# Nine-tap grouped convolutions by phases: the last convolution's partial shifts as 32x32 tiles in float32

## The reference, cut to what matters

```python
x = x + conv9(x, w0, groups=4, pad=4) + ctx0(c)[:, :, None] + side[None, :, None]
x = x + mixed(x, c, mix1)   # per sample: (sum_k att[k] * W[k]) @ x + (att @ bias_k)[:, None]
x = x + mixed(x, c, mix2)   # att = softmax of a small gelu network of the condition c
x = x + conv9(x, w3, groups=4, pad=4) + ctx3(c)[:, :, None] + side[None, :, None]
```

## Time and profile before

| | us |
|---|---|
| median of 3 runs | 631.91 |
| lowest, highest | 631.85, 632.3 |
| the profiled execution, its time | 635.33 |
| its span from first to last instruction | 633.5 |
| TensorE busy in it | 622.8 |
| VectorE, ScalarE, GpSimd busy | 500.9, 338.2, 272.3 |

### The profile page before, as it was taken

How to read it: one execution, slowest core, us unless ns; L and a number is a source line. 1 busy time by engine, 2 the same in 40 slices (tenths; PEclk the granted TensorE clock), 3 DMA queues, 4 the chain that set the end, 5 groups by cost and what they waited for, 6 DMA issues and landing times.

```text
span 633.5 us, 26750 instructions
## 1 busy us (share of the span) xinstructions
PE 622.8 (98%) x11938; PEld 506.3 (80%) x11938; DVE 500.9 (79%) x1002; ACT 338.2 (53%) x626; POOL 272.3 (43%) x163
## 2 busy tenths in 40 slices
PE   8999999999999999999999999999999999999995
PEld 6888897777788777889877778777878877788874
DVE  6899777978777887887887887797877788788735
ACT  4665455555455456455456446555545545645534
POOL 4133454354355345355435345435435534534220
PEclk8999999999999999999999999999999999999998
DMA  8066665557765556775555776555776555655515
GB/s 244 24 188 215 203 211 177 204 163 225 232 207 156 190 176 199 232 232 158 173 191 175 232 232 182 158 202 162 223 232 208 155 190 176 201 169 168 161 76 201
DMA packets 50572, 118.84 MB, mean 188 GB/s; under 512 B 5621, under 2 KB 26282, under 8 KB 42714
## 3 DMA queue, kind: packets, MB, share of 16 engines
q1 hardware_dynamic: 49170, 116.04, 58.1%
q0 software_dynamic: 576, 1.26, 0.5%
q10 hardware_dynamic: 776, 0.89, 0.4%
HBM read 35.33 MB, written 33.55 MB: 109 GB/s over the span
## 4 chain that ended last, share of the span: by engine, by line
PE 96%; DMA 2%; DVE 1%; ACT 1%; issue 0%; ACTq 0%; DVEq 0%
PE ps L1068 45%; PE ps L1079 19%; PE ps L1090 16%; PE ps L1214 14%; PE ps L1192 1%; DMA out_sb<-in_L_cond_weight 1%; DMA out_planes<-out_taps 1%; ACT out_sb L740 1%; PE ps L1262 0%; PE ps L1185 0%; DVE out_taps L856 0%; DVE x_in L950 0%; DVE x_hi L993 0%; PE ps L1250 0%; PE ps L1302 0%
## 5 line engine op out<-in xcount | busy, mean ns | idle before, releaser
L513 POOL COPY out_sb<-out_planes 128x2048 f32<-128x2048 f32 x30 | 123.0, 4099 | 187.8 <-issue 162.0
L496 POOL COPY x_full<-x_in 128x2048 f32<-128x2048 f32 x29 | 117.1, 4038 | 113.9 <-DVE x_lo L822 110.1
L846 DVE SCALAR_TENSOR_TENSOR z_lo<-ps,bias_tab,z_hi 128x1024 fp32r<-128x1024 f32 x62 | 76.7, 1279 | 60.7 <-ACT z_hi L649 60.7
L1090 PE MATMUL ps<-x_full,taps_raw 32*32 32x512 f32 x2880 | 102.2, 598 | 0.0
L1068 PEld LDWEIGHTS ps<-z_hi,taps_hi 32*128 32x128 f32 x1488 | 71.0, 183 | 35.4 <-issue 25.1
L1068 PE MATMUL ps<-z_hi,taps_lo 32*128 32x512 f32 x1488 | 96.5, 387 | 0.0
L836 DVE SCALAR_TENSOR_TENSOR y_lo<-ps,bias_tab,y_hi 128x512 fp32r<-128x512 f32 x128 | 87.2, 744 | 10.2 <-ACT y_hi L639 10.2
L1068 PE MATMUL ps<-z_hi,taps_hi 32*128 32x512 f32 x1488 | 94.2, 396 | 0.0
L657 ACT ACTIVATE out_taps<-ps,bias_tab 128x512 f32<-128x512 f32 x62 | 39.3, 685 | 102.2 <-PE ps L1068 102.2
L1068 PE MATMUL ps<-z_lo,taps_hi 32*128 32x512 f32 x1488 | 90.3, 385 | 0.0
L1214 PE MATMUL ps<-y_hi,mix_w 32*128 32x512 f32 x1024 | 88.0, 385 | 0.0
(11 more groups left out here) (158 smaller groups left out, 831.0 us busy)
## 6 DMA issues: line engine op xcount, KB each, us to landing
x_in<-in_x SPq DMA_DIRECT2D x31, 1024.0 KB, 5.3
out_planes<-out_taps SPq DMA_DIRECT2D x122, 256.0 KB, 3.6
out<-out_sb SPq DMA_DIRECT2D x30, 1024.0 KB, 4.6
mix_w<-prod SPq DMA_DIRECT2D x124, 128.0 KB, 4.0
x_in<-in_x SPq DMA_DIRECT2D x2, 512.0 KB, 5.9
out<-out_sb POOLq DMA_DIRECT2D x2, 512.0 KB, 3.5
out<-x_full SPq DMA_DIRECT2D x7, 128.0 KB, 2.9
out_taps<-in_L_cond_weight SPq DMA_DIRECT2D x1, 512.0 KB, 5.8
```

The source lines that it names most:

```text
L496: pool.tensor_copy(row_order(t, d, x[:, :, home(t, d)]), x_order(t, d, x_in[t.par(d)][:, :])).then_inc(x_planed, 1)
L513: pool.tensor_copy(x_order(t, d, out_sb[t.par(d)][:, :]), row_order(t, d, out_planes[:, :, :]))\
L846: dve.scalar_tensor_tensor(out=z_home(t, 0)[1][:, 2 * h:2 * h + 2, home(t, 0)], in0=ps[:, k:k + 2, :], scalar=bias_tab[:, b, 2 * G:BIAS], ...
L1090: tile = pe.matmul(ps[rows(p), first_bank + g, :], taps_raw[l][rows(g), d - p, :], full[rows(g), d % PH, c:c + S], start=False, stop=(n == ...
```

## The change

The partial shifts of conv3 take the form that conv0 has had: 18 whole turns, then 48 matmuls of 32x32 tiles in float32, for samples 1 to 30. In detail:

- `z_full`, a third copy of z in float32, unsplit. ScalarE writes it from PSUM in `whole_z`: two activations of 128x1024, each after the z_lo of its half, then, after both, two edge copies (3 phases each) and `z_full_edged`. It stands in `edges_z` between z_hi's edges and z_lo's; those now cover one phase each instead of four.
- `conv3_mixed` takes the place of `conv3` for t >= 2: 12 whole turns (LATER is 12), the product, 6 whole turns, the 48 small matmuls. At t = 31 mix(31) stands after the 12 turns.
- In `conv0_mixed`, before the last two of the 18 whole turns, TensorE now waits for `z_lo_done` and `z_full_edged` of sample t-1.
- The columns of conv3's weight tiles are in phase order (32 p + o) where they were 4 o + p; so the relay DMA reads 32 neighbouring partitions for each phase where it read every fourth.
- Sample 31 (`last_conv`) keeps the old column order. It needs its own tiles: after conv0(31) GpSimd zeroes `taps_hi[0]` and `taps_lo[0]` whole, ScalarE and VectorE fill them from `taps_raw[1]` (four instructions each, `last_taps_high` ahead of z_hi(31), `last_taps_low` ahead of z_lo(31)). Its bias is moved to the old order by four small DMAs of GpSimd at t = 16.

```diff
+        def full_z(t, d):
+            return not isinstance(t.half, int) or FIRST_FULL_Z <= t.i + d < N - 1
...
-                    sp.dma_start(out_planes[:, p, :], out_taps[p:C:PH, :, :]).then_inc(out_relaid, DMA)
+                    sp.dma_start(out_planes[:, p, :], out_taps[rows(p), :, :]).then_inc(out_relaid, DMA)
...
+            def zero_last_taps():
+                pool.wait_ge(conv0_done, G * N)
+                for w in (taps_hi[0], taps_lo[0]):
+                    pool.memset(w[:, :, :].bitcast(F32), 0.0).then_inc(last_taps_zeroed, 1)
...
             def edges_z(t):
                 for z, done in ((z_hi, z_hi_done), (z_lo, z_lo_done)):
+                    if z is z_lo and full_z(t, 0):
+                        whole_z(t)
                     act.wait_ge(done, 2 * (t.i + 1))
-                    for o, i in edges(z):
+                    for o, i in (edges(z, slice(PH - 1, PH), slice(0, 1)) if full_z(t, 0) else edges(z)):
                         last = act.activation(o, i.bitcast(F32), ACT.Copy)
                 last.then_inc(z_edged, 1)
+
+            def whole_z(t):
+                b = t.i
+                for h in range(2):
+                    act.wait_ge(z_lo_done, 2 * b + h + 1)
+                    k = bank(t, 0) + 2 * h
+                    act.activation(z_full[:, 2 * h:2 * h + 2, home(t, 0)], ps[:, k:k + 2, :], ACT.Identity,
+                                   bias=bias_tab[:, b, 2 * G:BIAS]).then_inc(z_full_done, 1)
+                act.wait_ge(z_full_done, 2 * (b + 1 - FIRST_FULL_Z))
+                for o, i in full_edges(z_full):
+                    last = act.activation(o, i, ACT.Copy)
+                last.then_inc(z_full_edged, 1)
...
-                whole_turns(bank(t, 0), 0, hi, lo, [(2, d) for d in far], step, False)
+                pe.wait_ge(z_lo_done, 2 * b)
+                pe.wait_ge(z_full_edged, b - FIRST_FULL_Z)
+                if t.at(2):
+                    pe.wait_ge(taps_raw_step[1], 2)
+                whole_turns(bank(t, 0), 0, hi, lo, [(2, d) for d in far], step)
                 if middle:
                     middle()
-                partial_turns(bank(t, 0), 0, full, conv0_done, step)
+                partial_turns(bank(t, 0), 0, full, step, done=conv0_done)
+
+            def conv3_mixed(t, turns, middle):
+                b = t.i - 1
+                order = [(k, d) for k in range(2) for d in WHOLE] + [(2, d) for d in WHOLE]
+                if t.at(2):
+                    pe.wait_ge(prod_summed, b + 2)
+                pe.wait_ge(z_edged, b + 1 - PLAIN)
+                whole_turns(bank(t, -1), 1, z_hi, z_lo, order[:turns], BLK, first=True)
+                middle()
+                whole_turns(bank(t, -1), 1, z_hi, z_lo, order[turns:], BLK)
+                partial_turns(bank(t, -1), 1, z_full, BLK, done=conv3_done)
...
-            MID = TURNS // 2
-            LATER = 20
+            LATER = 12
...
+                elif t.at(N - 1):
+                    conv3_mixed(t, LATER, lambda: mix(t))
+                else:
+                    conv3_mixed(t, LATER, lambda: product(t, 1))
                     mix(t)
```

More of the change, by code:

```diff
@@ L46 @@
 FIRST_MIXED = 2
+FIRST_FULL_Z = 1
 K = 8
@@ L85, in conditioned_residual_kernel @@
         z_lo = sb("z_lo", [C, PH, ROW], F32R)
+        z_full = sb("z_full", [C, PH, ROW])
         out_taps = sb("out_taps", [C, G, S])
@@ L372, in phase_columns, with last_columns @@
         def phase_columns(w, l, p):
-            view = w[l][:, p:p + TAPS, :]
-            return view[:, :, GC * p:GC * p + GC] if l == 0 else view[:, :, p:C:PH]
+            return w[l][:, p:p + TAPS, GC * p:GC * p + GC]
+        def last_columns(w, p):
+            return w[0][:, p:p + TAPS, p:C:PH]
         def rows(r):
@@ L580, in _ @@
                 pool.memset(buf[:, :, ROW - 1:ROW].bitcast(F32), 0.0).then_inc(far_zeroed, 1)
-            for buf in x_full:
+            for buf in x_full + [z_full]:
                 pool.memset(buf[:, :, 0:ROW:ROW - 1], 0.0).then_inc(far_zeroed, 1)
@@ L584, in _, with bias_for_last @@
             first_planes(ALL[1], 1)
+            def bias_for_last():
+                pool.wait_ge(bias_tab_done, 3)
+                for p in range(PH):
+                    pool.dma_start(bias_last[p:C:PH, :], bias_tab[rows(p), N - 1, G:2 * G]).then_inc(bias_last_in, DMA)
+            def zero_last_taps():
+                pool.wait_ge(conv0_done, G * N)
+                for w in (taps_hi[0], taps_lo[0]):
+                    pool.memset(w[:, :, :].bitcast(F32), 0.0).then_inc(last_taps_zeroed, 1)
             for t in ALL[2:N]:
@@ L587, in _ @@
                     end_rows(t.i - 1)
+                if t.i == N // 2:
+                    bias_for_last()
                 one(t)
+            zero_last_taps()
             store_woven(0)
@@ L664, in taps_high, with last_taps_high @@
                    .then_inc(taps_hi_done[l], 1)
+            def last_taps_high():
+                act.wait_ge(last_taps_zeroed, 2)
+                for p in range(PH):
+                    act.activation(last_columns(taps_hi, p), taps_raw[1][:, :, :], ACT.Copy).then_inc(last_taps_hi_done, 1)
             def spread_first():
@@ L719, in relay_last @@
                 for p in range(2, PH):
-                    act.dma_start(out_planes[:, p, :], out_taps[p:C:PH, :, :]).then_inc(out_relaid, DMA)
+                    act.dma_start(out_planes[:, p, :], out_taps[rows(p), :, :]).then_inc(out_relaid, DMA)
             def evac_last(h):
+                act.wait_ge(bias_last_in, PH * DMA)
                 for g in range(2, G):
@@ L940, in one, with last_taps_low @@
                     low_z(t)
+            def last_taps_low():
+                dve.wait_ge(last_taps_zeroed, 2)
+                for p in range(PH):
+                    dve.wait_ge(last_taps_hi_done, p + 1)
+                    dve.tensor_tensor(out=last_columns(taps_lo, p), in0=taps_raw[1][:, :, :],
+                                      in1=last_columns(taps_hi, p).bitcast(F32), op=ALU.subtract)\
+                       .then_inc(last_taps_lo_done, 1)
             def turn_last(h):
@@ L956, in bias_first_half @@
             def bias_first_half():
+                dve.wait_ge(bias_last_in, PH * DMA)
                 for g in range(2):
@@ L1071, in conv_turns, with whole_turns @@
                             tile.then_inc(done, 1)
-            def whole_turns(first_bank, l, hi, lo, turns, step, first):
+            def whole_turns(first_bank, l, hi, lo, turns, step, first=False, done=None):
                 for k, d in turns:
@@ L1078, in whole_turns, with partial_turns @@
                     for g in range(G):
-                        pe.matmul(ps[:, first_bank + g, :], w[rows(g), d, :], a[rows(g), d % PH, c:c + S],
-                                  start=(first and (k, d) == turns[0]), stop=False)
-            def partial_turns(first_bank, l, full, done, step):
+                        tile = pe.matmul(ps[:, first_bank + g, :], w[rows(g), d, :], a[rows(g), d % PH, c:c + S],
+                                         start=(first and (k, d) == turns[0]), stop=(done is not None and (k, d) == turns[-1]))
+                        if done is not None and (k, d) == turns[-1]:
+                            tile.then_inc(done, 1)
+            def partial_turns(first_bank, l, full, step, first=False, done=None):
                 for n in range(PARTIAL):
@@ L1090, in partial_turns @@
                             tile = pe.matmul(ps[rows(p), first_bank + g, :], taps_raw[l][rows(g), d - p, :],
-                                             full[rows(g), d % PH, c:c + S], start=False, stop=(n == PARTIAL - 1))
-                        if n == PARTIAL - 1:
+                                             full[rows(g), d % PH, c:c + S], start=(first and n == 0),
+                                             stop=(done is not None and n == PARTIAL - 1))
+                        if done is not None and n == PARTIAL - 1:
                             tile.then_inc(done, 1)
@@ L1104, in conv0_mixed @@
                 wait(pe, out_dve, 2 * (b - 1))
-                whole_turns(bank(t, 0), 0, hi, lo, [(k, d) for k in range(2) for d in near], step, True)
+                whole_turns(bank(t, 0), 0, hi, lo, [(k, d) for k in range(2) for d in near], step, first=True)
                 if not plain(t, 0):
                     pe.wait_ge(x_hi_edged, b + 1 - PLAIN)
-                whole_turns(bank(t, 0), 0, hi, lo, [(k, d) for k in range(2) for d in far], step, False)
+                whole_turns(bank(t, 0), 0, hi, lo, [(k, d) for k in range(2) for d in far], step)
                 if not plain(t, 0):
```

31 lines of the change are left out of this document (21 added, 10 removed).

## The result

The changed kernel takes 726.12 us (725.49 to 727.36, 3 runs) against 631.91; the ratio is 1.149, with a 95% interval of 1.147 to 1.151. It is 94 us slower, where 71 more were forecast; the range was 690 to 745.

A forecast was written before the change was run, and what follows sets the result against it. TensorE bounds the kernel, busy 622.8 of 633.5 us. Step 2 3.8, steps 3 to 30 64.7, step 31 2.2 and the relay 0.5 sum to 71.2; with 631.91, 703.1 us, range 690 to 745.

The forecast's parts named there:

- The two stalls: TensorE idles in each step, 2.17 us inside conv0 for z_full and 0.62 us at the product for y_lo.
- TensorE's own work: conv3 loses 18 turns and gains 48 small matmuls: 0.48 us a step less, 18.34 us from 18.82.
- The wait inside conv0: Before conv0's last two whole turns, TensorE stands from 3.63 to 5.80 us until z_full is complete: 2.17 us a step.
- The product's wait: In conv3, TensorE reaches the product at 12.57 us but y_lo allows it at 13.19: 0.62 us.
- The step, 21.13: Loop step from one conv0 start to the next: 21.13 us, 2.31 more than 18.82.
- Beginning: Step 2 costs 3.8 us more; from step 3 on, each step costs 2.31 us more.
- End: Step 31, conv0 to last_conv, takes 20.87 us, 2.2 more; the last relay takes 0.5 more.
- new tiles for sample 31: Tiles refilled after the last conv0 are ready by 15.5, ahead of z at 16: no cost, up to 1 us.
- The clock: TensorE's granted clock stays up, near 0.99, with both stalls: 52%, 692 to 715 us; its fall: 32%.
- a clock under 0.97: Sign in the profile afterwards that the forecast is wrong: TensorE's granted clock below 0.97.
- rival 1: TensorE's clock falls in the stalls, one step in two, 1.7 to 3.4 us each: 720 to 755 us, 32%.
- Rival 2: z_full's wait in conv0 is met in time, only the product is late: step 19.93, 664 us; about 10%.

The follow-up runs named there:

- run 3: Changed kernel with the z_full wait moved from conv0 to conv3 (except step 2) and the product behind all 18 whole turns; 628.82 us, ratio 0.995.
- run 8: Kernel before, with only the relay changed to read 32 neighbouring partitions for each phase; 633.31 us, ratio 1.0014.
- run 11: run 3 with sample 1 keeping conv3's old turns and the last relay's four DMAs shared out in another order; 627.58 us, ratio 0.993.
- run 10: Changed kernel with eight extra matmuls of 128x128x512 ahead of the wait in conv0, output not the reference's; 709.27 us.
- run 1: Changed kernel with TensorE waiting for z_full in conv3 and not inside conv0, step 2 keeping its wait; 669.49 us, ratio 1.060.
- run 4: Changed kernel with one more wait in conv0, four whole turns earlier, for the first half of z_full; 725.28 us.
- run 5: run 3 with the parts of the next sample's matrices behind y_hi and y_lo on ScalarE and VectorE; 658.28 us.

## Why the prediction was right or wrong, point by point

The measured time lies in the range, but not where the forecast had its centre: 726.1 against 703.1. The two stalls came as they were worked out; on top of them the clock fell, which the prediction had as its first rival, and the range held because that rival was in it. Of the 23 us between, some 18 are the falls, 3 the step, 1 step 3 and 1.6 the end behind `last_conv`.

- *TensorE's own work becomes 18.34 us a step.* Right: run 3 measured 18.52, with the product 0.13 late by its own timeline.
- *The wait inside conv0, resuming at 5.80.* Right, 5.79. The stall is 1.96 to 2.01 by the trace's idle time against the 2.17 of the working, since the modelled end of the matmul ahead of it lies inside the stall. What follows is P at 6.46 where 6.37 was worked out: two turns and the passage take 0.67 behind a stall, not 0.57.
- *The product's wait.* Right in kind and place: product at 13.21 against 13.19. Its idle time is 0.35, not 0.62, for the same reason.
- *The step, 21.13.* The quiet steps are 21.19 to 21.35, 21.25 on average. Over 28 steps the difference is some 3 us.
- *Beginning.* Step 2 cost 3.7 us (3.8 forecast), step 3 cost 3.2 (2.31). In step 3 z_hi starts 1.26 us after conv0 in place of 0.24: ScalarE stands at x_lo's edges until 72.62, because x_lo of step 2 is late, and conv0's stall is 2.98 us.
- *End.* conv0(31) to `last_conv` took 22.41, which is 20.9 and one fall; 20.87 was forecast. The relay was taken at 0.5 more; it is longer by 2.7 in the trace, of which run 8 accounts for 1.9, and the end behind `last_conv` is longer by 2.1. The estimate from the port rate that the Trainium skill gives for 32 neighbouring partitions ("SBUF — State Buffer", Door 1: The DMA port swizzle) had been some 2 us more, and these traces, 1.9 and 2.7, agree with it in size. The new tiles for sample 31 were hidden here; in the faster runs 3 and 11 they aren't: `last_conv` waits 0.7 and 1.3 us for z_lo(31), which stands behind them on VectorE.
- *The clock.* This is the step that failed. The forecast gave the clock staying up 52% and its fall 32%; the clock fell in 12 of 30 steps. The prediction named a clock under 0.97 as a sign of being wrong, and the profiled execution had 0.967 (the other two 0.970 and 0.965). As a size, rival 1 had half the steps at 1.7 to 3.4 us each; they were 12 at 1.5, hence 18 us where 25 to 51 stood. Run 10, with both delays kept and the clock up, is the nearest to what the forecast described: 709.3 against 703.1. The working counted the length of one gap against the gaps of 1.2 and 0.3 us in the earlier trace rows and then let the density of the rest decide; runs 1 and 4 show that neither one long gap nor any gap at all is the criterion. What is, stays open. The rule cited from the Trainium skill ("TensorE: Matmul & The Clock Gate", Why this matters for your kernels), by which only longer gaps than these matter, does not hold here: the gaps were 2.0 us in the changed kernel, and 1.0 and 0.7 in run 4.
- *Rival 2, 664 us.* It didn't happen, but run 1 made it by hand: 669.5, with the step of 19.93 met.

## What to carry to other kernels

A wait that is put early in the instruction stream for a later reader stalls all the work in between: read, for every new wait, at what time of the step its releaser is ready, and put it where that has passed. When an instruction stream is shortened, the waits inside it come earlier too; a margin of 0.37 us was gone with eight turns taken from ahead of the product. And an idle engine can cost twice: here TensorE stood for 2.3 us in a quiet step, and a falling clock cost another 18 us on top.

## What the hardware showed

- Idle time of 2.0 us in a step of 21 brought TensorE's clock down in 12 of 30 steps; 1.0 and 0.7 us close together did so 14 times, 1.3 us alone never in the loop (run 1), and the same steps with the gap filled by full matmuls never in the loop (run 10). What triggers a fall stays open.
- The profiled execution of before had its clock down in the stretch 10 to 20 us (0.66). TensorE had stood for 1.2 and 0.3 us between 5 and 10. The profiled execution of run 8, the same code but for the relay, had it at 1.00 there and no such gaps; conv0(2) started at 48.15 in place of 51.65. These 3.5 us fit the 3.4 by which the profiled execution of before, 635.33, stood above its median.
- A cast of 128x128 on VectorE took 1.87 us in place of 0.23 beside a 4 us copy on GpSimd and ended just behind it (run 5; the median of its 32 casts is 1.89, in run 3 it is 0.23).
